# Bias products moved into the waits of the agents' chain, two more sets of products of ones, another order of loads, new sequences

## The chip, the core and the metric

The kernel runs on one NeuronCore of a Trainium2 chip. The metric is the device time of one execution in microseconds, and lower is better. TensorE (PE) multiplies matrices, with a separate instruction to load the weights (PEld). VectorE (DVE), ScalarE (ACT) and GpSimd (POOL) work on vectors. SyncE (SP) issues every load and store to one DMA queue. Each engine runs its own list of instructions in order. The engines wait for one another, and for loads, by semaphores.

## What is computed

The reference takes x (32 sequences of 100 tokens with 256 features), a context (32 x 361 x 256) and two masks. It runs six layers, each added to its input and followed by a layer norm:

```
x = LN(x + agent_attention(x))           # "agents": a softmax over features, one over tokens, all 32 sequences
x = LN(x + cross_attention(x, ctx))      # "first", masks added as logarithms
x = LN(x + top_half_attention(x))        # "pick": gates, the 50 best tokens, 16 heads
x = LN(x + banded_attention(x))          # "local": 16 heads, biases a_bq, a_bk, a_bv, a_bo
x = LN(x + cross_attention(x, ctx))      # "second": biases c_bq, c_bk, c_bv, c_bo
x = LN(x + int8_projection(quant(x)))    # "quant"
```

Everything is in float32 but the last product. Because biases meet only weights, some products depend on constants alone and are computed once at the start:

- for the second cross attention, `wqk` = c_qT · c_kT and `wvo` = c_vT · c_o (the combined weights), and `wqbk`, `bqbk`, `bqk` from c_bk and c_bq (the first bias products);
- `bo1` = a_bv · a_o + a_bo (the second bias product) and `bvo` = c_bv · c_o + c_bo (the third).

## The kernel before

The 32 sequences are 16 pairs. Four streams, A to D, each take one pair per turn, in four turns. A stream has its own tiles in SBUF and two of the eight PSUM banks. Within a turn it goes through the stages mix, first, pick, local, second and quant. Each engine has one generator per stream (`tensor_turns`, `vector_turns`, `scalar_turns`, `gpsimd_turns`, `sync_turns`). A string in `ORDER` (from line 1410), one per engine, says whose step comes next. Each letter advances that stream's generator to its next `yield`. So the order of work on every engine is written out by hand or by a planner, and an engine that meets a wait in its list holds back everything behind it.

Ahead of the turns stands the agent attention of all sequences: `tensor_agents`, `vector_agents`, `scalar_agents`. It is one serial chain. Tokens arrive in eight slots of four sequences (`ld_x`). For each slot TensorE transposes the tokens (line 362, semaphores x0 to x15), VectorE multiplies them with w (line 878, ag0 to ag7), and TensorE adds the weighed tokens of the slot before (`weighed`, line 331). From the sums y comes a row (yr1), its columns (line 337, yT1), the key product with w_k0 (line 375), a softmax over features (kmax, kexp, krec, kn), its transposes (line 380, arT), a product with w_v0 (z), the logits over tokens (line 394, log), their exponentials (lexp) and transposes (col), weighed tokens again (u), columns (yT2), and the product with w_v0T (line 411, vec). VectorE scales this to `agent_v`, semaphore v (line 922).

Where TensorE would wait in this chain, `idle(n)` (line 343) lets it compute n products of ones that nobody reads. Each is 256 columns wide and is recorded as two passes. They stand ahead of the tokens, three before kn, two before lexp, one before yr2, and one at the end.

The first turn of C and D opens with the constants' products in `tensor_turns` (C: first bias products, `wqk`; D: second and third, `wvo`). VectorE takes them out of PSUM (lines 978 to 991), with the semaphore "bias" of `s.tensor["start"]` and `s.vector["start"]`, for which ScalarE's q of the second cross attention and three steps of GpSimd wait as well. After that, four rows of `agent_v` are spread for each stream's pair (line 511), for which mix waits.

`sync_first` issues the loads in this order: w_q0, the tokens, w_k0, w_v0 and w_v0T (`ld_wk`), all other constants of the start (`ld_c`), x_k and x_o, masks of A and B, x of all streams, masks of C and D, contexts of A and B, the constants of the later stages (`ld_const`, 16 transfers), then after u the contexts of C and D, whose rooms held tokens, and after v the store of `agent_v`.

Of the kernel before, what the change touches and what calls it, by code (L numbers as in the profile page):

```python
# [15 lines left out]
P = 128  # L16
# [33 lines left out]
class Steps:  # L50
# [8 lines left out]
    def up(self, name):  # L59
# [46 lines left out]
AGENT_TENSOR = "zero w " + " ".join(f"x{n}" for n in range(16)) + " y yT1 key arT z log col u sum yT2 vec"  # L106
AGENT_SCALAR = " ".join(f"x{n}" for n in range(16)) + " toke kexp lexp"
AGENT_VECTOR = ("ones zero w " + " ".join(f"ag{n}" for n in range(8)) + " tokd yr1 yT1 kmax krec kn aT zT tokr tok lmax acol acol2 "
                "yr2 rsum yT2 v")
# [10 lines left out]
def program(nc, ins, out):  # L120
    ctx = ExitStack()
    with ctx:
# [117 lines left out]
        for s in streams[0:2]:  # L240
            s.tensor["start"] = Steps(s.tensor["start"].sem, "rows")

# [49 lines left out]
        ld_w0, ld_wk, ld_c, ld_first, ld_const = (sem(n) for n in ("ld_w0", "ld_wk", "ld_c", "ld_first", "ld_const"))  # L292
# [33 lines left out]
        def tensor_agents(e):  # L326
# [13 lines left out]
            def idle(n):  # L340

                for _ in range(n):
                    e.matmul(psum[0:S, 2, 0:D], ones[:, :], ones[:, 0:1].to_broadcast([P, D]), start=True, stop=True)

            e.wait_ge(*agent_dve("ones"))
            idle(1)
# [5 lines left out]
            idle(1)  # L352
# [16 lines left out]
            weighed(7, SLOTS - 1, token_w).then_inc(*agent_pe.up("y"))  # L369
            e.wait_ge(*agent_dve("yr1"))  # L370
# [6 lines left out]
            idle(3)  # L377
# [4 lines left out]
            e.wait_ge(*agent_dve("aT"))  # L382
            for h in range(NC):
# [5 lines left out]
            e.wait_ge(*agent_act("x15"))  # L389
# [7 lines left out]
            idle(2)  # L397
# [8 lines left out]
            idle(1)  # L406
# [6 lines left out]
            idle(1)  # L413

        def tensor_turns(e, s):
# [71 lines left out]
            for t in range(TURNS):  # L487
                if t == 0:

                    if s is SC_:  # L490
                        e.wait_ge(ld_c, LD_C)
                        spread(e, bk[0][:, 0:D], cols["c_bk"], W["c_qT"])
                        for c in range(NC):
                            e.matmul(bk[0][:, D:D + 1], cols["c_bk"][:, c:c + 1].to_broadcast([P, P]), cols["c_bq"][:, c:c + 1],
                                     start=c == 0, stop=c == NC - 1)
                        for h in range(NC):
                            last = columns(bk[0][:, D + 1 + h:D + 2 + h], W["c_kT"], h, lambda c: cols["c_bq"][:, c:c + 1])
# [202 lines left out]
        def scalar_turns(e, s):  # L700
# [16 lines left out]
            def cross(t, stage, bq):  # L717
# [3 lines left out]
                if t == 0 and bq is not None:  # L721
                    e.wait_ge(*SC_.vector["start"]("bias"))
# [136 lines left out]
        def vector_agents(e):  # L859
# [49 lines left out]
            e.tensor_tensor(tok[:, :], toke, tokr, ALU.mult).then_inc(*agent_dve.up("tok"))  # L909
            e.wait_ge(*agent_pe("log"))  # L910
# [3 lines left out]
            e.tensor_copy(acol.rearrange("p (i j) -> p i j", j=ROWS), batches(psum[0:S, 7, 0:P])).then_inc(*agent_dve.up("acol2"))  # L914
            e.wait_ge(*agent_pe("u"))
# [3 lines left out]
            batch_columns("yT2")  # L919
            e.wait_ge(*agent_pe("vec"))  # L920
# [3 lines left out]
        def vector_turns(e, s):  # L924
# [50 lines left out]
            for t in range(TURNS):  # L975
                if t == 0 and s is SC_:
                    e.wait_ge(*s.tensor["start"]("bias"))
                    e.tensor_scalar(wqbk[:, :], bk[0][:, 0:D], INV, None, ALU.mult)
                    e.tensor_scalar(bqbk[:, :], bk[0][:, D:D + 1], INV, None, ALU.mult)
                    e.tensor_scalar(bqk[:, :], bk[0][:, D + 1:D + 1 + NC], INV, None, ALU.mult).then_inc(  # L980
                        *s.vector["start"].up("bias"))
                elif t == 0 and s is SD:
                    e.wait_ge(ld_c, LD_C)
                    e.wait_ge(*s.tensor["start"]("bias"))
                    e.tensor_scalar(bq4[:, :], cols["a_bq"][:, :], HEAD_SCALE, None, ALU.mult)
                    e.tensor_copy(w8[:, :, :], w8_i)
                    e.tensor_tensor(bo1[:, :], bk[0][:, 0:D], rows["a_bo"], ALU.add)
                    e.tensor_tensor(bvo[:, :], bk[0][:, D:2 * D], rows["c_bo"], ALU.add).then_inc(*s.vector["start"].up("bias"))
# [205 lines left out]
        def gpsimd_turns(e, s):  # L1194
# [30 lines left out]
            for t in range(TURNS):  # L1225
# [17 lines left out]
                else:  # L1243
                    e.wait_ge(*SD.vector["start"]("bias"))
# [6 lines left out]
                if t == 0:  # L1251
                    e.wait_ge(ld_const, LD_CONST)
                    e.wait_ge(*SD.vector["start"]("bias"))
# [9 lines left out]
                if t == 0:  # L1263
                    e.wait_ge(*SC_.vector["start"]("bias"))
# [40 lines left out]
        def sync_first(e):  # L1305
# [16 lines left out]
            for n in COLVECS[1:]:  # L1322
# [15 lines left out]
            load_ctx(e, SB_, 0)  # L1338
            for n in ("f_q", "f_k", "f_v", "f_o", "a_q", "a_k", "a_v"):
# [7 lines left out]
            e.wait_ge(*agent_pe("u"))  # L1347
            for s in (SC_, SD):
                load_ctx(e, s, 0)
# [62 lines left out]
        "BACDABABCBCADADBCBAABDCAACABCDCBCBDADDACDDABABCAABBACADCBBACDABBCACDBDCBCABCDDADCBDAADACBDBDAACBACAC"  # L1412
        "DCBDBCABDDBCACBACBDCBABCCBCDADCDACDBABCADBCDABACADCBCADBCABDDABDCDADBADAAAADABCBBDBCBBABABCCDCDCCDCC"
        "BAABADDDADADBDBACCAABBABBCCDBDBCABACACACCDCCDAABDBBDCBABBADDDCDDACBCADBACDCDBDCBCABDDCACADBADCADBDBA"
        "BCDACCBADCACBBDBDCADBCDCABCABDADBCDBAACDABCADBDCABDCABCADCABBCBDDAACBADCADCAABCBAABABCDDCDBBBDBCBDAA"
        "DCCDCCBBCDACADDDAADDBAACACBAABBBBBBCDCDBACAACACCCCDCDBADBABDBACDDDDADCBBACACBDCCADBDCBDBACBDDCADCABD"
        "ACDBBCDADBCBAACACDBACBDBDCBACADCADBBCBADDBDCAADCABCABDDCBDAABCADBCADCDCBADBACCBACADBCABAAAADDBCBBDCD"
        "BBABBCACCDDCCDCABCBADADADDAADDCACABABBBBBBDCDCBACABACACDCCCCDAABDBABDDBCADDDDABBCACBCBDCABDCDBDACCBD"
        "DCAACBDADCADBDAABDACBCABDCCBCBDBADACDCBCDACBBADDBDACBCADACBBADCDABDABACCDCABCBDDBDCABCADCADCABDAAAAA"
        "BCDBCDBCBBBBACDCBDACDCCCDDDDDDBBCCDD"),  # L1420
    "DVE": (
        "BACBDCDCADABAABCBCCAADABDDACBABADCBCBDDCBCAACAAADADBABDACBABBBCBABCCBDCCCCDBDCDDADDDADAACBADABCBAABC"
        "DCBCBACBBDCADCCBABACDBCDCDBACDADBCAABDCABCBACDACABCDDBDBBDDDAAACDCAADABABBADBDBBCCACACBBCDCBDCDAABAD"
        "DCDCADABBCBDABDABACABCCDACABCCBABDCACDDABBACBABBDADBDCADDBCDACBCBDCCCDCBDCDDAADDDAADCBDABCBABCABACCD"
        "BDCBDCBADACBCADABDBACBDADCAABDCCBDABCBADACADBCCBDBBAADCACCDCDAABBADBDDBDBAABACCCBADBCBDCDCBADCAADCDA"
        "CDAABBBCDABBADACCBCDAACBCBCBDCDAAACDCADBBDAADBABDBDCCDCBBBACBDCDCCCBDCDDADDDCADBAADBCABACBACBACBDCBA"
        "BDCADBDCBACDABDABDDCACABDACCBDABBADADCACDBCCDBBBCACAADDCCAAABDBBDDAABDBBCCACBACBCDBCDADBAACDCDDACAAD"
        "CBBBDADABACDCBACBCCABCBABDCDACADCABDAADBDABBDBCDBCBBDABCCDCCDCCBDDCADDDADCAADBADABCBABCACBCDBADCBBCD"
        "DACBCADABDBCABDADCABACDCBADBACDDBCACBDBCDCBDDCAAACADAABDBADBCCABCBBABDCDCCDBDDDBCDCDCD"),
    "ACT": (  # L1430
        "ABBAABCDACCBABADBCABDCACCBDBACDDCDAADBADBCACBABADADBCCAABBACDDBBCCADCBACDABDDCABDAABDCACDCDBCBABBDAA"
        "CCCDBBDBCCACDAADCBBCBDDCADAABCCCABBADDAADBABDDABAAACDCBBACABBBCBACDCDDCBCADBCADABAADCDBDACADABBCABDB"
        "CDBBCCBBDCAACCADCACDACBDBDDCABCDBBDADABDBCCADCDABDDCBACDBCACDADBCABDDBACDACCABDBCDBBACDCDACABBDBDCDA"
        "CAACBBDBDDAACCABCABBDDADCACAACBAABABCADBBCBDCDBBAABDCCDADBBCCDACDCBDAADBDAACDACBAABCDABDBBCBBBACCDAC"
# [101 lines left out]
```

## Time and profile before

| what | value |
|---|---|
| runs | 853.36, 854.22, 847.25 us |
| median | 853.36 us |
| the profiled execution | 853.0 us |
| its span in the trace | 851.1 us |
| busy: PE, DVE, ACT, POOL | 92%, 77%, 57%, 42% of the span |
| mean granted clock of TensorE | 0.97 of full speed |
| chain that ended last | PE 64%, DVE 16%, POOL 8%, ACT 7% |
| DMA | 53.31 MB, mean 63 GB/s |

The profiled execution lies 0.4 us below the median. Its span leaves out 1.9 us around the recorded instructions. A busy share is an average over the whole run: the share of the first stretches differs from that of the rest, so it is read stretch by stretch. The granted clock is the share of TensorE's full clock (2.4 GHz) that it was given.

### The profile page before, as it was taken

To read this page: it belongs to the slowest core of one execution; us is meant where nothing else is said; L and a number is where in the kernel's file an instruction comes from. 1 tells how busy PE (TensorE), PEld (TensorE's weight loads), DVE (VectorE), ACT (ScalarE), POOL (GpSimd) and SP (SyncE) were. 2 spreads that over 40 slices of the span, in tenths; PEclk is the share of its full clock that TensorE was granted. 3 is DMA by queue.
4 is the path that set the end of the run, shared out by engine and by line. 5 is a ranking of instruction groups with operands and counts; after the bars stand their busy time and mean duration, and the time that the engine had idled before them with its cause. 6 is when DMAs were issued, how large, how long until landed. Compare 5 with 4: busy or idle time off the path is not lost.

```text
span 851.1 us, 20772 instructions
## 1 busy us (share of the span) xinstructions
PE 785.4 (92%) x8013; PEld 606.1 (71%) x8013; DVE 654.7 (77%) x1973; ACT 488.7 (57%) x1509; POOL 359.3 (42%) x604
## 2 busy tenths in 40 slices
PE   8989999998887999999989899999999899999992
PEld 4566787765766778766767688776777688777771
DVE  6163888787787698788778779789769879888676
ACT  3126445686556445577655554588655645587654
POOL 0088312306676523403775632402777633202465
PEclk7799999999999999999999999999999999999996
DMA  9893000001353000000236000001244200000001
GB/s 222 240 288 154 2 2 2 1 3 56 113 191 135 23 2 2 1 3 29 97 134 220 29 12 2 1 2 29 60 170 154 78 2 2 2 2 2 2 1 39
DMA packets 23074, 53.31 MB, mean 63 GB/s; under 512 B 3888, under 2 KB 9680, under 8 KB 22976
## 3 DMA queue, kind: packets, MB, share of 16 engines
q1 hardware_dynamic: 22976, 51.99, 19.1%
q8 instruction: 63, 1.03, 0.5%
q14 instruction: 35, 0.29, 0.1%
HBM read 48.67 MB, written 3.31 MB: 61 GB/s over the span
## 4 chain that ended last, share of the span: by engine, by line
PE 64%; DVE 16%; POOL 8%; ACT 7%; issue 3%; DMA 1%; SPq 0%; DVEq 0%; ACTq 0%; POOLq 0%
PE psum L429 11%; PE psum L434 11%; PE psum L473 8%; PE psum L630 5%; PE psum L652 5%; PE psum L459 4%; PE psum L643 4%; DVE bn L930 2%; ACT x L710 2%; POOL rstd L1199 2%; PE psum L466 2%; PE psum L565 2%; POOL xplus L1206 1%; PE psum L424 1%; PE psum L574 1%
## 5 line engine op out<-in xcount | busy, mean ns | idle before, releaser
L710 ACT ACTIVATE x<-res,ez,rstd 100x256 f32<-100x256 f32 x160 | 86.7, 593 | 65.4 <-POOL ez L1202 65.2
L473 PE MATMUL psum<-eT,ctx 128*128 128x100 f32 x768 | 95.2, 280 | 1.3 <-DVE eT L956 1.3
L473 PEld LDWEIGHTS psum<-eT,ctx 128*128 128x128 f32 x768 | 92.4, 197 | 2.5 <-DVE eT L956 1.7
L1197 POOL TENSOR_SCALAR ve<-mv 100x2 f32<-100x2 f32 x96 | 22.4, 233 | 163.2 <-DVE mv L933 159.1
L704 ACT ACTIVATE eT<-psum 100x400 f32<-100x400 f32 (+3 forms) x128 | 61.7, 495 | 43.7 <-PE psum L466 19.5
L459 PE MATMUL psum<-ctxT,qT 128*100 128x361 f32 x256 | 84.9, 474 | 1.5 <-ACT qT L704 1.1
L816 ACT ACTIVATE work<-psum,mx 100x100 f32<-100x100 f32 x256 | 67.5, 365 | 21.7 <-DVE mx L1112 21.5
L1185 POOL TENSOR_TENSOR kT<-cell,kT 100x722 f32<-100x722 f32 x12 | 20.7, 1722 | 131.5 <-ACT cell L684 131.5
L704 ACT ACTIVATE xT<-psum 128x400 f32<-128x400 f32 (+2 forms) x80 | 35.5, 445 | 69.0 <-PE psum L589 25.7
L1199 POOL TENSOR_TENSOR rstd<-ve,minus_half 100x2 f32<-100x2 f32 x96 | 70.1, 730 | 8.0
L930 DVE BATCH_NORM_STATS2 bn<-res 100x6 f32<-100x256 f32 x192 | 71.2, 412 | 0.0
L822 ACT ACTIVATE work<-psum,mx 100x100 f32<-100x100 f32 x256 | 67.9, 383 | 3.7 <-DVE mx L1115 3.6
L643 PE MATMUL psum<-ident,work 100*100 100x100 f32 x512 | 60.8, 255 | 3.1 <-ACT work L822 1.8
L459 PEld LDWEIGHTS psum<-ctxT,qT 128*100 128x100 f32 x256 | 41.3, 168 | 31.2 <-ACT qT L704 1.8
L1122 DVE RECIPROCAL xT<-psum 128x100 f32<-128x100 f32 x64 | 49.6, 776 | 14.6 <-PE psum L652 14.1
L1202 POOL TENSOR_SCALAR ez<-mv,rstd 100x1 f32<-100x1 f32 x192 | 52.9, 291 | 9.5
L643 PEld LDWEIGHTS psum<-ident,work 100*100 100x100 f32 x512 | 45.7, 128 | 14.6 <-issue 4.1
L466 PE MATMUL psum<-ident,work 100*128 100x100 f32 x192 | 29.0, 264 | 16.2 <-ACT work L741 15.8
L1112 DVE TENSOR_REDUCE mx<-psum 100x4 f32<-100x400 f32 x64 | 36.0, 568 | 9.3 <-PE psum L635 9.2
L1216 POOL COPY work<-rden 128x256 f32<-128x256 f32 x16 | 6.4, 398 | 84.2 <-DVE rden L1072 84.1
L1119 DVE COPY eT<-psum 100x400 f32<-100x400 f32 x64 | 35.8, 566 | 6.9 <-PE psum L643 6.4
L466 PEld LDWEIGHTS psum<-ident,work 100*128 100x128 f32 x192 | 20.8, 144 | 27.2 <-ACT work L741 23.9
(243 smaller groups left out, 2028.1 us busy)
## 6 DMA issues: line engine op xcount, KB each, us to landing
ctx<-in_ctx SPq DMA_DIRECT2D x16, 768.0 KB, 7.0
ctxT<-in_ctxT SPq DMA_DIRECT2D x16, 722.0 KB, 5.0
cell<-in_cell SPq DMA_DIRECT2D x12, 282.0 KB
seq<-in_seq SPq DMA_DIRECT2D x12, 282.0 KB
x<-in_x SPq DMA_DIRECT2D x16, 200.0 KB
out<-vs SPq DMA_DIRECT2D x16, 200.0 KB
eT<-agent_rows SPq DMA_DIRECT2D x12, 200.0 KB
work<-in_x SPq DMA_DIRECT2D x4, 384.0 KB
```

What stands on the lines that cost most here:

```text
L429: last = e.matmul(dst, w[:, c, h * P:(h + 1) * P], n(c), start=c == 0, stop=c == NC - 1)
L434: last = e.matmul(dst, xT(c), w[:, c, :], start=c == 0, stop=c == NC - 1)
L459: last = e.matmul(bk[b][0:S, 0:S2], s.qT[:, c, b * S:(b + 1) * S], s.ctxT[:, b, c, :], start=c == 0, stop=c == NC - 1)
L466: last = e.transpose(bk[b][:, j * S:(j + 1) * S], s.p[:, b, j * P:(j + 1) * P], ident[0:S, 0:S])
L473: last = e.matmul(bk[b][:, c * S:(c + 1) * S], s.ctx[:, b, j, c * P:(c + 1) * P], s.pT[:, b, j, :], start=j == 0, stop=j == S2C - 1)
L643: last = e.transpose(bk[g][0:S, q * S:(q + 1) * S], s.e[:, 4 * g + q, :], ident[0:S, 0:S])
L704: return e.activation(dst, src, ACT.Copy, **kw)
L710: e.activation(dst[0:S, b, :], s.res[0:S, b, :], ACT.Identity, scale=s.rstd[:, b:b + 1], bias=s.shift[:, b:b + 1]).then_inc(*act.up(f"x{b}"))
L816: last = e.activation(s.e[:, h, :], bk[0][0:S, h % 4 * S:(h % 4 + 1) * S], ACT.Exp, bias=s.mx[0:S, h:h + 1])
L822: last = e.activation(s.e[:, h, :], bk[1][0:S, h % 4 * S:(h % 4 + 1) * S], ACT.Exp, bias=s.mx[0:S, h:h + 1])
L930: e.bn_stats(s.bn[:, b, :], s.res[0:S, b, :]).then_inc(*dve.up(f"bn{b}"))
L1199: e.tensor_tensor(s.rstd[:, :], s.vare[:, :], minus_half[0:S, 0:NB], ALU.pow).then_inc(*pool.up("rstd"))
```

## The change

- `bias_c`, the first bias products, moves from C's first step into the wait for kn, in PSUM bank 4. It replaces three products of ones. The wait for x15 moves ahead of it. VectorE takes the results out after `tok`, semaphore cb.
- The second bias product moves from D's first step into the wait for lexp (bank 2, replacing two products of ones, semaphore ab). The third moves into the wait for yr2 (bank 3, replacing one, semaphore vb). VectorE does the casts and additions that belong to them after acol2 and after yT2.
- C and D keep the combined weights and the rows. The waits for "bias" are replaced by waits for cb, ab and vb.
- Two products of ones are added in the first slot, between its transposes and those of the second, and one between y and yr1.
- The loads: c_bq, c_bk, c_qT and c_kT (`ld_cb`) come directly behind w_k0, then w_v0 and w_v0T (`ld_wv`), then the rest of `ld_c`. The contexts of C and D, with their wait for u, come ahead of the constants of the later stages.
- All five strings of `ORDER` are new. They have the same lengths. A stream's n-th step moves by at most 7 places on PE, 5 on DVE, 8 on ACT, 7 on POOL and 3 on SP. POOL's first 20 steps are the same.

```diff
-            def idle(n):
+            def idle(n, bank):
...
+            def bias_c():
+                spread(e, psum[:, 4, 0:D], cols["c_bk"], W["c_qT"])
+                for c in range(NC):
+                    e.matmul(psum[:, 4, D:D + 1], cols["c_bk"][:, c:c + 1].to_broadcast([P, P]), cols["c_bq"][:, c:c + 1],
+                             start=c == 0, stop=c == NC - 1)
+                for h in range(NC):
+                    for c in range(NC):
+                        last = e.matmul(psum[:, 4, D + 1 + h:D + 2 + h], W["c_kT"][:, c, h * P:(h + 1) * P],
+                                        cols["c_bq"][:, c:c + 1], start=c == 0, stop=c == NC - 1)
+                last.then_inc(*agent_pe.up("cb"))
...
-                if i:
+                if i == 0:
+                    idle(2, 2)
+                else:
                     e.wait_ge(*agent_dve(f"ag{i - 1}"))
                     weighed(7, i - 1, token_w)
             e.wait_ge(*agent_dve("ag7"))
             weighed(7, SLOTS - 1, token_w).then_inc(*agent_pe.up("y"))
+            idle(1, 2)
             e.wait_ge(*agent_dve("yr1"))
...
-            idle(3)
+            e.wait_ge(ld_cb, LD_CB)
+            e.wait_ge(*agent_act("x15"))
+            bias_c()
             e.wait_ge(*agent_dve("kn"))
...
             e.wait_ge(*agent_dve("aT"))
+            e.wait_ge(ld_wv, LD_WV)
...
-            idle(2)
+            e.wait_ge(ld_c, LD_C)
+            spread(e, psum[:, 2, 0:D], cols["a_bv"], W["a_o"]).then_inc(*agent_pe.up("ab"))
             e.wait_ge(*agent_act("lexp"))
...
-            idle(1)
+            spread(e, psum[:, 3, 0:D], cols["c_bv"], W["c_o"]).then_inc(*agent_pe.up("vb"))
             e.wait_ge(*agent_dve("yr2"))
...
+                    e.wait_ge(*agent_dve("v"))
                     if s is SC_:
-                        e.wait_ge(ld_c, LD_C)
-                        spread(e, bk[0][:, 0:D], cols["c_bk"], W["c_qT"])
...
-                        last.then_inc(*s.tensor["start"].up("bias"))
                         weights(W["c_qT"], W["c_kT"])
                     elif s is SD:
-                        e.wait_ge(ld_c, LD_C)
-                        e.wait_ge(*agent_dve("v"))
-                        spread(e, bk[0][:, 0:D], cols["a_bv"], W["a_o"])
-                        spread(e, bk[0][:, D:2 * D], cols["c_bv"], W["c_o"]).then_inc(*s.tensor["start"].up("bias"))
                         weights(W["c_vT"], W["c_o"])
-                    if s in (SC_, SD):
-                        e.wait_ge(*s.vector["start"]("bias"))
-                    e.wait_ge(*agent_dve("v"))
...
-            for n in ("w_k0", "w_v0", "w_v0T"):
-                weight(n, ld_wk)
-            for n in ("a_o", "c_qT", "c_o", "c_kT", "c_vT"):
+            weight("w_k0", ld_wk)
+            for n in ("c_bq", "c_bk"):
+                e.dma_start(cols[n][:, :], ins[n]).then_inc(ld_cb, 16)
+            for n in ("c_qT", "c_kT"):
+                weight(n, ld_cb)
+            for n in ("w_v0", "w_v0T"):
+                weight(n, ld_wv)
+            for n in ("a_o", "c_o", "c_vT"):
                 weight(n, ld_c)
...
+            e.wait_ge(*agent_pe("u"))
+            for s in (SC_, SD):
+                load_ctx(e, s, 0)
             for n in ("f_q", "f_k", "f_v", "f_o", "a_q", "a_k", "a_v"):
                 weight(n, ld_const)
...
-            e.wait_ge(*agent_pe("u"))
-            for s in (SC_, SD):
-                load_ctx(e, s, 0)
...
-        "BACDABABCBCADADBCBAABDCAACABCDCBCBDADDACDDABABCAABBACADCBBACDABBCACDBDCBCABCDDADCBDAADACBDBDAACBACAC"
+        "BACDABBABCCDADABCADCABAACACBBCBDBDCADDACDDABABCAABCABADCBBACABBDCACDBDCABCBDDCACDBDAADACBDBADABCACAD"
...
```

## Rows read from the trace of the kernel before

**Rows 1.** The page, busy time of one engine over the span.
```profile
PE 785.4 (92%) x8013; PEld 606.1 (71%) x8013; DVE 654.7 (77%) x1973; ACT 488.7 (57%) x1509; POOL 359.3 (42%) x604
```

**Rows 2.** Busy time by stretch: us, each engine's busy time, granted clock, DMA.
```profile
4.27:7.69 3.42, 2.17 (x12) 1.28 (x11) 0.80 (x4) 0.00 (x0) 0.00 (x0) 1.00 1.05 248
7.69:11.10 3.41, 1.98 (x23) 1.17 (x22) 2.65 (x17) 1.80 (x4) 0.00 (x0) 1.00 1.06 234
11.10:28.17 17.07, 16.51 (x106) 8.99 (x106) 9.38 (x50) 6.17 (x13) 0.00 (x0) 0.50 0.99 253
28.17:31.58 3.41, 3.10 (x7) 1.53 (x8) 0.75 (x3) 0.56 (x2) 0.00 (x0) 0.50 0.61 203
45.45:57.27 11.82, 11.82 (x58) 8.92 (x58) 7.67 (x24) 2.07 (x4) 8.85 (x12) 1.00 0.94 297
57.27:72.62 15.35, 11.84 (x60) 8.30 (x60) 8.76 (x25) 9.07 (x24) 14.57 (x17) 1.00 0.82 295
72.62:93.00 20.38, 20.38 (x137) 17.08 (x138) 10.62 (x41) 10.70 (x34) 11.93 (x13) 1.00 0.09 30
93.00:837.13 744.13, 698.57 (x7375) 546.83 (x7373) 601.70 (x1763) 451.96 (x1418) 315.68 (x545) 0.99 0.13 45
```

**Rows 3.** Chain of waits, agents' chain: start us, us, what was waited for.
```profile
25.10 1.87 PE psum L331 x16
...
27.47 0.70 PE psum L337 x2
...
28.48 1.92 PE psum L375 x4
30.39 2.09 PE psum L343 x6
...
37.45 1.04 PE psum L343 x4
...
43.85 1.05 PE psum L411 x4
```

**Rows 4.** Timeline of the token slots: start us, us, instructions, idle time before them.
```profile
9.24 0.91 PE L362 MATMUL psum<-ident,work 100*128 100x100 f32 x8 [1.09 <-DMA work<-in_x]
...
21.50 0.08 DVE L878 DVE_READ_ACCUMULATOR x<-ctxT,vs 100x1 f32 x1
```

**Rows 5.** Chain of waits, first steps of C and D.
```profile
47.43 1.06 PE psum L323 x4
48.49 0.34 PE psum L494 x4
48.83 2.73 PE psum L429 x16
...
52.59 1.92 PE psum L323 x8
54.51 1.73 PE psum L429 x8
```

**Rows 6.** Timeline around the start of the streams, four instructions.
```profile
44.94 0.47 DVE L922 TENSOR_SCALAR agent_v<-psum,vs 32x256 f32<-32x256 f32 x1 [1.14 <-PE psum L411]
...
54.73 1.08 ACT L710 ACTIVATE x<-res,ez,rstd 100x256 f32<-100x256 f32 x2
...
63.93 2.60 PE L459 MATMUL psum<-ctxT,qT 128*100 128x361 f32 x8
...
71.52 0.54 DVE L943 CUSTOM_DVE_ANT_0 work<-psum,kT 100x361 f32<-100x361 f32 x1 [0.16 <-POOL kT L1185]
```

**Rows 7.** Timeline of SyncE's issues: the load of c_kT, B's context.
```profile
14.74 2.90 SPq L1307 DMA_DIRECT2D xplus<-in_c_kT  x1
...
38.00 0.49 SPq L1302 DMA_DIRECT2D ctx<-in_ctx  x1
```

**Rows 8.** The same two issues in the DMA view: KB, us to landing.
```profile
xplus<-in_c_kT SPq DMA_DIRECT2D x1, 256.0 KB, 9.4
...
ctx<-in_ctx SPq DMA_DIRECT2D x1, 768.0 KB, 20.0
```

More of the change, by code:

```diff
@@ L103 @@
 }
-AGENT_TENSOR = "zero w " + " ".join(f"x{n}" for n in range(16)) + " y yT1 key arT z log col u sum yT2 vec"
+AGENT_TENSOR = "zero w " + " ".join(f"x{n}" for n in range(16)) + " y yT1 key cb arT z log ab col u sum vb yT2 vec"
 AGENT_SCALAR = " ".join(f"x{n}" for n in range(16)) + " toke kexp lexp"
-AGENT_VECTOR = ("ones zero w " + " ".join(f"ag{n}" for n in range(8)) + " tokd yr1 yT1 kmax krec kn aT zT tokr tok lmax acol acol2 "
-                "yr2 rsum yT2 v")
+AGENT_VECTOR = ("ones zero w " + " ".join(f"ag{n}" for n in range(8)) + " tokd yr1 yT1 kmax krec kn aT zT tokr tok cb lmax acol acol2 "
+                "ab yr2 rsum yT2 vb v")
 def take(order, programs):
@@ L241, in program @@
             s.tensor["start"] = Steps(s.tensor["start"].sem, "rows")
+        for s in streams[2:4]:
+            s.tensor["start"] = Steps(s.tensor["start"].sem, "weights rows")
+            s.vector["start"] = Steps(s.vector["start"].sem, "weights")
         def job_before(s, t):
@@ L290, in program @@
         psum = ctx.enter_context(nc.psum_tensor("psum", [P, 8, 512], F32))
-        ld_w0, ld_wk, ld_c, ld_first, ld_const = (sem(n) for n in ("ld_w0", "ld_wk", "ld_c", "ld_first", "ld_const"))
+        ld_w0, ld_wk, ld_wv, ld_cb, ld_c, ld_first, ld_const = (
+            sem(n) for n in ("ld_w0", "ld_wk", "ld_wv", "ld_cb", "ld_c", "ld_first", "ld_const"))
         ld_x = [sem(f"ld_x{k}") for k in range(SLOTS)]
@@ L338, in columns_of_rows @@
                 return last
-            def idle(n):
+            def idle(n, bank):
                 for _ in range(n):
-                    e.matmul(psum[0:S, 2, 0:D], ones[:, :], ones[:, 0:1].to_broadcast([P, D]), start=True, stop=True)
+                    e.matmul(psum[0:S, bank, 0:D], ones[:, :], ones[:, 0:1].to_broadcast([P, D]), start=True, stop=True)
+            def bias_c():
[8 more added lines that the diff above has]
+                last.then_inc(*agent_pe.up("cb"))
             e.wait_ge(*agent_dve("ones"))
-            idle(1)
+            idle(1, 2)
             e.wait_ge(*agent_dve("zero"))
@@ L351, in tensor_agents @@
             last.then_inc(*agent_pe.up("zero"))
-            idle(1)
+            idle(1, 2)
             e.wait_ge(ld_w0, LD_W0)
@@ L369, in tensor_agents @@
             weighed(7, SLOTS - 1, token_w).then_inc(*agent_pe.up("y"))
+            idle(1, 2)
             e.wait_ge(*agent_dve("yr1"))
@@ L412, in tensor_agents @@
             last.then_inc(*agent_pe.up("vec"))
-            idle(1)
+            idle(1, 5)
         def tensor_turns(e, s):
@@ L721, in cross @@
                 if t == 0 and bq is not None:
-                    e.wait_ge(*SC_.vector["start"]("bias"))
+                    e.wait_ge(*agent_dve("cb"))
                 e.wait_ge(*pe("q", t))
@@ L914, in vector_agents @@
             e.tensor_copy(acol.rearrange("p (i j) -> p i j", j=ROWS), batches(psum[0:S, 7, 0:P])).then_inc(*agent_dve.up("acol2"))
+            e.wait_ge(ld_c, LD_C)
+            e.tensor_scalar(bq4[:, :], cols["a_bq"][:, :], HEAD_SCALE, None, ALU.mult)
+            e.tensor_copy(w8[:, :, :], w8_i)
+            e.wait_ge(*agent_pe("ab"))
+            e.tensor_tensor(bo1[:, :], psum[:, 2, 0:D], rows["a_bo"], ALU.add).then_inc(*agent_dve.up("ab"))
             e.wait_ge(*agent_pe("u"))
@@ L919, in vector_agents @@
             batch_columns("yT2")
+            e.wait_ge(*agent_pe("vb"))
+            e.tensor_tensor(bvo[:, :], psum[:, 3, 0:D], rows["c_bo"], ALU.add).then_inc(*agent_dve.up("vb"))
             e.wait_ge(*agent_pe("vec"))
@@ L975, in vector_turns @@
             for t in range(TURNS):
[L976 to L988, printed above, removed]
                 if t == 0 and s in (SC_, SD):
@@ L1243, in gpsimd_turns @@
                 else:
-                    e.wait_ge(*SD.vector["start"]("bias"))
+                    e.wait_ge(*agent_dve("vb"))
                 e.memset(s.v_pick[:, :, :, :], 0.0).then_inc(*s.gpsimd["pick"].up("zero"))
@@ L1252, in gpsimd_turns @@
                     e.wait_ge(ld_const, LD_CONST)
-                    e.wait_ge(*SD.vector["start"]("bias"))
+                    e.wait_ge(*agent_dve("ab"))
                 add_row(s.gpsimd["local"], s.scalar["pick"], t, bo1)
@@ L1263, in gpsimd_turns @@
                 if t == 0:
-                    e.wait_ge(*SC_.vector["start"]("bias"))
+                    e.wait_ge(*agent_dve("vb"))
                 add_row(s.gpsimd["second"], s.scalar["local"], t, bvo)
@@ L1321, in sync_first @@
                 e.dma_start(rows[n], ins[n].to_broadcast([P, D])).then_inc(ld_c, 16)
-            for n in COLVECS[1:]:
+            for n in ("a_bq", "a_bk", "a_bv", "c_bv"):
                 e.dma_start(cols[n][:, :], ins[n]).then_inc(ld_c, 16)
@@ new lines @@
+    "ACT": (
+        "ABABBACBCACDDACBABDACADCBADCBDCDBACADBBDACACDABDBACAABCABCBDABDCBACCBADCDABDADCBDBAADACCCDBCDABADBBA"
+        "CDCCBBBDCCCAADDABCCBCBDDAAABDCCCABBADDADABABDDAADAACBBCBCAABBBBACDCCDDCABCCBDADBAAADCDBDACADABCBADBB"
+        "DCBBBCCCDBAACDCACABCDCADBDDACBDCBADABCDDBBCADBCDADBDCADCCBACBDDADBACDBACBDAACCCDBDBBADCDACACBBDBDCDC"
+        "AABCADBDBDAACCABCBDABDACAADABCCAABBACABBDCBDCDBCBACADBDADBBCCDACDBCAADDABDACADCBAABCDABBDBCBBBACCDAC"
+        "CACCADBCCDADBDDCDBDCABADADBCABDBCDACDBCDBCABDCACDABDACBDDBCDCACABADBCBDACBDADCACBBBDDCDAAACCBDBDBADA"
+        "ACCBBCADBDADCACAABCBABADAACDBBCBCDBAABBCDCDACDBBDCACCADBAADABDACDCDAAABCBDDBCBBBABBCDCACCDACACDDCACB"
+        "BDDCABDCBDDBAADACDBBDCACBDDCBACCDBACDABDACBDADBAADCBCCDDBCBBACDACADCBBDDBCDAACACBBDBDADAACCCBBDDBDCA"
+        "CACAADBDAAABADCBCBBAACBCBCBDCDACDBDCBDADDDCCBDDCDBCD"),
```

61 lines of the change are left out of this document (25 added, 36 removed).

## The prediction

> **What bounds the kernel now.** I read the page first. TensorE is busy 785.4 of 851.1 us, 92% of the span [rows 1], so an edit counts if it takes work off TensorE or closes one of its 65.7 us of gaps. Then I asked for busy time by stretch, because the change touches the first 60 us and only reorders the rest. Three kinds of stretch stand there [rows 2]. Up to 45.45 us TensorE serves one serial chain of small steps (the agents' chain). From 11.10 to 31.58 the granted clock is 0.50, that is 1.2 GHz instead of 2.4, although TensorE is busy 16.51 of 17.07 us in the longest part of it. From 45.45 to 57.27 it is busy without a gap, from 57.27 to 72.62 it idles 15.35 - 11.84 = 3.51 us while GpSimd is busy 14.57 of 15.35, and from 72.62 to 93.00 it has no gap at all. After that it idles 744.13 - 698.57 = 45.6 us in 744, 6%. Third, the chain of waits gives the serial steps one by one [rows 3, 5]; the timeline gives the one wait for tokens that the change fills [rows 4]; two rows of other engines say what the start-up of the four streams hangs on [rows 6]; and the loads say when weights and contexts are there [rows 7, 8].
>
> The sum is made against the profiled execution: 853.0 us, span 851.1. The median of the runs shown is 853.36, so 0.4 us comes on top. Those runs go from 847.25 to 854.22: 1% (8.5 us) is about what a measurement of this kernel can tell from no change.
>
> **The change, part by part.**
>
> 1. Two products of ones in the first wait for tokens. One such product takes 1.04 / 2 = 0.52 us at full clock (two of them, the group at 37.45) [rows 3]; two make 1.04 us, and the wait they fill is 1.09 us [rows 4]: nothing is pushed back. What they might buy is the clock. Before it fell at 11.10, TensorE was busy 1.98 of 3.41 us, nearly all of it transposes of tokens and one set of weighed sums; one stretch earlier, with the products for w in it, it was busy 2.17 and kept full clock [rows 2]. After the fall it stayed at half for 17.07 us at 97% busy. So being busy with this mixture (a slot's transposes, then a set of weighed sums, the last two sets 1.87 us together at half clock [rows 3]) does not bring the clock back, and I see no reason why the same mixture, which leaves the engine less busy at full clock, should hold it. Two products come once; the mixture goes on for seven more slots. I take 0 for this part. The bound on the other side is the whole clock, and is rival one.
>
> The Trainium skill, "TensorE: Matmul & The Clock Gate", "Why this matters for your kernels", advises leaving no long idle gaps between bursts of matmuls so that the clock stays up; by that rule the filled wait keeps it and the result is the time of rival one. The trace speaks against this rule as the whole cause: the clock fell with no gap above 1.09 us ahead of it, and stayed down at 97% busy. The same page, "Part 4: PE-mode transpose", says that a transpose does not count as busy for the clock in the way a matmul does; that fits the row, and by it the products would have to outweigh the transposes of every slot.
>
> 2. One product of ones between y and the first column transposes. At half clock it takes 1.04 us; y ends at 25.10 + 1.87 = 26.97 and the transposes start at 27.47 [rows 3], so it pushes them to 28.0, +0.53. It may also let the clock return sooner. Before, the clock came back at 31.58, after the key product (1.92 at half clock) and the products of ones that start at 30.39. If it returns with the added product, at about 28.2: transposes 28.0 to 28.6, then 0.31 for VectorE (27.47 + 0.70 to 28.48), then the key product at full clock, 1.05 as its twin at 43.85 [rows 3], ends at 29.98. If it returns at 31.58 as before, the key product ends at 28.0 + 0.70 + 0.33 + 1.92 = 30.95.
>
> 3. The first bias products (`bias_c`) replace three products of ones (2.09 us, 30.39 to 32.48 [rows 3]) in the wait for kn. Their price at full clock: 1.06 + 0.34 + (2.73 - 1.73) = 2.40 us; the 2.73 holds the small products and the combined weights together, and 1.73 is the same combined-weight group alone, at 54.51 [rows 5]. Early return: 29.98 + 2.40 = 32.38, no later than before (-0.1). Late return: 0.6 us of it at half clock, the end at 33.68, +1.2. VectorE's three scalings follow while TensorE does transposes and logits, ahead of a maximum that is needed only once the logits are done.
>
> 4. The second (`ab`) replaces two products of ones, 1.04 us, by one pair, 1.06: 0. It waits for the other constants, whose loads of before were done when TensorE used them at 47.43 without a gap. The third (`vb`) replaces one product by 1.06: +0.54 if what follows had been waiting on the product rather than on VectorE, 0 if not; I take +0.54 [rows 3, 5]. VectorE's casts and additions lie under the weighed sums for u and the transposes behind them.
>
> 5. New waits on loads. c_kT landed at 14.74 + 9.4 = 24.1 [rows 7, 8]; now a_o and c_o are behind it and two 1 KB columns ahead. Nothing asks for it before 29.98. w_v0 and w_v0T slip behind it and are asked for after 32. Nothing paid; a whole weight's delay would still be covered.
>
> So agent_v, ready at 44.94 + 0.47 = 45.4 before [rows 6], comes between -0.1 + 0.54 = +0.4 and +1.2 + 0.54 = +1.7 us later. I take +1.1, the middle, since no row says when the clock returns.
>
> 6. After agent_v. Streams C and D lose their bias products: 2.40 and 1.92 us, 4.32 in all [rows 5]. The fourth stream's rows end 7.5 us after agent_v, not 11.8. But the first stage needs x of A and B, and ScalarE delivers it at 54.73 + 1.08 = 55.81 [rows 6], 10.4 after agent_v, whatever TensorE does: at that point only 57.27 - 55.85 = 1.4 of the 4.3 us is gained. GpSimd, 95% busy from there to 72.62 [rows 2], sets the softmax of the other stream (VectorE waited for its mask sum at 71.52 [rows 6]). What TensorE does ahead then counts, because it is the bound from 72.62 to 93.00. Contexts of C and D now come before the constants, so their scores can be drawn into the gaps. Bounds: 0 (everything hangs on GpSimd) and 4.3; I take 2.9, the middle between 1.4 and 4.3, nearer the upper end because a stretch of 20 us without a gap follows. The contexts wait for u behind those of A and B, as before; what is queued behind that wait are constants that the second stage is the first to use. The store of agent_v is still last: nothing paid.
>
> 7. The new sequences move steps by at most 7 places on TensorE, 5 on VectorE, 8 on ScalarE. Worth 0 by itself; bounds by the idle time they can act on, a tenth of 45.6: 4.6 us either way, of which I let 3 into the forecast's own range.
>
> **Sum.** 853.0 + 1.1 - 2.9 = 851.2, and 851.6 with the 0.4. Its own range: from 853.4 + 0.4 - 4.3 - 3 = 846.5 to 853.4 + 1.7 - 0 + 3 = 858.1.
>
> **The rivals.**
>
> *The clock holds through the tokens.* Then y is bound by arrivals: VectorE ends its last slot at 21.6 [rows 4]; one set of weighed sums (half of 1.87, and half of that again at full clock) later it is 22.1, 4.9 us ahead of 26.97. The column transposes gain 0.3 and the key product 0.87; `vb` costs 0.54, and `bias_c` about 0.3 over the products it replaces (2.40 - 2.09). agent_v is 4.9 + 0.3 + 0.87 - 0.84 = 5.2 us earlier. Then a load binds: the context of B lands at 38.00 + 20.0 = 58.0 [rows 7, 8], and its scores, at 63.93 before [rows 6], can gain 5.9, no more; what is done meanwhile for C and D can still gain up to 5.2 + 4.3 = 9.5 by work. I take the middle, 7.7: 845.7. For: the products fall where TensorE had its last long gap before the fall, and 847.25 among the runs before shows that something worth 6 us can go the other way. Against: rows 2. Chance 0.2.
>
> *The bias products lengthen the chain and give nothing back.* Place: the wait for kn, with the clock still down. At half clock `bias_c` is 4.8 us, 2.7 above the 2.09 replaced; with 0.53 and 0.54, agent_v is 3.8 us late. If GpSimd then sets the pace and only 1.4 us comes back: 853.4 + 3.8 - 1.4 = 855.8. It decides once agent_v is later than 45.4 + 2.9. For: GpSimd at 95%; added work where TensorE is slowest. Against: dense products brought the clock back at 31.58. Chance 0.15.
>
> *The sequences decide.* Fitted to the new state, they close a tenth of the later gaps and all of the 4.3 shows: 853.4 + 1.1 - 4.3 - 4.6 = 845.6, chance 0.1. Ill fitted by the same tenth: 853.4 + 1.1 - 2.9 + 4.6 = 856.2, chance 0.05.
>
> The forecast keeps 0.5.
>
> **Numbers.** The range takes the forecast's case but for its ends, half of rival one and most of rival two: 845 to 857. Faster by over 1%, below 844.8: the lower half of rival one with good sequences, 0.08. Slower by over 1%, above 861.9, needs rival two and bad sequences: 0.04. Within 1%: 0.88.
>
> **What would show it.** Step 1: the granted clock between 11 and 27 us; above 0.6 there I am wrong on the cause. Step 2: the end of the half-clock stretch, 28.2 or 31.6, and the start of the key product. Step 3: the transposes of the normalised key start between 32.4 and 33.7. Step 6: agent_v between 45.8 and 47.1, the last of the four rows 7.5 us behind it, then a gap of about 2.9 us until x is there; idle time of TensorE between there and 93. Step 7: TensorE's idle time after 93, against 45.6. The prediction is wrong if agent_v moves by over 2 us either way, or if the later idle time changes by over 5.

## The result, and the profile after

The changed kernel took 855.96 us (median of 20 runs, 851.17 to 860.13), the kernel before 852.33 us (20 runs, 844.65 to 858.68). The ratio is 1.006, interval 1.0037 to 1.0082: 0.6% slower. A ratio leaves out the executions that took over 1.5% more than the fastest of their kernel; medians and means take in all. The forecast was 851.6 us, a little faster. The time lies inside the range and within the 1% that was called the likeliest; the sign is wrong.

The profiled execution took 855.3 us, span 853.5. The page first, the engines' busy time:

```profile
PE 784.3 (92%) x8007; PEld 608.6 (71%) x8007; DVE 656.0 (77%) x1973; ACT 489.4 (57%) x1509; POOL 358.1 (42%) x604
```

TensorE is busy 1.1 us less and idle 3.5 us more than in [rows 1]. The busy time by stretch, columns as in [rows 2]:

```profile
4.27:7.69 3.42, 3.42 (x14) 2.21 (x13) 0.39 (x1) 0.04 (x1) 0.00 (x0) 1.00 1.00 258
7.69:11.10 3.41, 3.15 (x32) 2.21 (x29) 3.38 (x20) 1.93 (x5) 0.00 (x0) 1.00 1.06 257
11.10:28.17 17.07, 14.21 (x131) 8.66 (x130) 10.26 (x53) 6.00 (x15) 0.00 (x0) 0.98 1.00 259
28.17:31.58 3.41, 3.00 (x66) 2.73 (x70) 1.21 (x7) 0.00 (x0) 0.00 (x0) 0.50 0.63 184
45.45:57.27 11.82, 9.75 (x41) 7.11 (x40) 9.12 (x29) 3.34 (x7) 9.68 (x13) 0.90 1.03 356
57.27:72.62 15.35, 12.80 (x59) 9.02 (x59) 6.35 (x16) 10.83 (x31) 14.73 (x16) 0.97 0.69 236
72.62:93.00 20.38, 20.38 (x152) 17.73 (x151) 12.99 (x52) 9.19 (x28) 10.12 (x16) 1.00 0.09 29
93.00:837.13 744.13, 697.87 (x7345) 546.20 (x7343) 596.98 (x1742) 450.39 (x1410) 311.58 (x534) 0.99 0.13 45
```

From 11.10 to 28.17 the clock is 0.98 where it was 0.50, and TensorE, faster, is now less busy (14.21 us instead of 16.51). Then it is at half from 28.17 on. Here is the chain of waits of the agents' chain (start us, us, what was waited for), to be read against [rows 3]:

```profile
21.27 0.62 PE psum L335 x8
21.89 0.61 PE psum L347 x2
22.50 0.39 PE psum L341 x2
...
24.25 1.06 PE psum L327 x4
25.31 0.34 PE psum L352 x4
25.64 0.89 PE psum L356 x8
...
28.99 5.52 PE psum L414 x128
34.51 1.06 PE psum L327 x4
```

y is ready at 21.9 and not at 27.0. The bias products cost 1.06 + 0.34 + 0.89 = 2.29 us (2.40 foreseen). The logits (L414) then take 5.52 us at half clock. In the kernel before this row stood:

```profile
34.51 2.93 PE psum L394 x128
```

Two rows of the timeline give the end of the chain and the first product of the pick stage, the first work that needs the late constants:

```profile
42.33 0.47 DVE L940 TENSOR_SCALAR agent_v<-psum,vs 32x256 f32<-32x256 f32 x1 [0.81 <-PE psum L432]
...
87.19 0.42 DVE L1025 SCALAR_TENSOR_TENSOR work<-x,f_wg_r 100x256 f32<-100x256 f32 x1
```

The second of them in the kernel before:

```profile
90.33 0.43 DVE L1020 SCALAR_TENSOR_TENSOR work<-x,f_wg_r 100x256 f32<-100x256 f32 x1 [0.78 <-ACT x L710]
```

agent_v is there at 42.8 us, 2.6 earlier than in [rows 6]; the pick product starts 3.1 us earlier. So between these two profiles the start won 3 us, and the end is 2.4 us later by the two spans: 5.5 us are lost after 87 us. The idle time of TensorE after 93 us is nearly the same in the two profiles (46.3 and 45.6 us of a fixed stretch), so that count, which I had named as the sign to look at, does not show the loss: work that is late simply falls out of the stretch at its end. The timeline of SyncE's issues does show something, around 262 us:

```profile
260.04 0.35 SPq L1305 DMA_DIRECT2D ctxT<-in_ctxT  x1
260.44 0.43 SPq L1307 DMA_DIRECT2D ctx<-in_ctx  x1
260.91 0.36 SPq L1295 DMA_DIRECT2D eT<-agent_rows  x1
261.31 0.41 SPq L1305 DMA_DIRECT2D ctxT<-in_ctxT  x1
261.76 0.55 SPq L1307 DMA_DIRECT2D ctx<-in_ctx  x1
262.35 0.45 SPq L1295 DMA_DIRECT2D eT<-agent_rows  x1
262.91 0.31 SPq L1292 DMA_DIRECT2D x<-in_x  x1
```

The contexts of D and C (1.5 MB each) go out back to back, and C's x directly behind them. The kernel before, same view:

```profile
246.44 0.33 SPq L1300 DMA_DIRECT2D ctxT<-in_ctxT  x1
246.81 0.43 SPq L1302 DMA_DIRECT2D ctx<-in_ctx  x1
...
264.60 0.28 SPq L1287 DMA_DIRECT2D x<-in_x  x1
264.93 0.35 SPq L1300 DMA_DIRECT2D ctxT<-in_ctxT  x1
```

There C's context left at 246.44, and x led D's context. In the changed kernel SyncE stood still meanwhile. Its own waits from 215 to 285 us have this row, the wait of a context's load for D's second attention, over at 260 us:

```profile
SPq L1305 <- PE psum L494: 10.9, 1, 10.9
```

The chain of waits of the changed kernel goes on from there:

```profile
262.77 0.14 DVE work L1164
262.91 10.95 DMA x<-in_x
...
273.88 0.88 DVE res L1010 x2
```

x lands 10.95 us after its issue, and VectorE's mix waits for it. The same pattern stands at 434 us with B's context ahead of A's. In the view of waits from 100 to 837 us the kernel before has no wait for x at all; the changed one has this row:

```profile
DVE res L1010 <- DMA x<-in_x: 2.6, 2, 1.8
```

VectorE idles only 2.6 us for it, in two places, because it has other streams' steps to do first. The stream itself starts its turn late; what that costs in the end the row does not say, the experiments do.

### The profile page after: what moved, and what is told of

It reads as the page before. It is cut to its first block, busy times and chain, and to the rows that moved or that the text cites. A ratio compares the mean times of both kernels' runs of the same rounds, so it can differ in the third digit from the quotient of the medians.

```text
span 853.5 us, 20757 instructions
## 1 busy us (share of the span) xinstructions
PE 784.3 (92%) x8007; PEld 608.6 (71%) x8007; DVE 656.0 (77%) x1973; ACT 489.4 (57%) x1509; POOL 358.1 (42%) x604
## 4 chain that ended last, share of the span: by engine, by line
PE 65%; DVE 15%; POOL 6%; ACT 6%; DMA 4%; issue 2%; SPq 1%; DVEq 0%; ACTq 0%; POOLq 0%
PE psum L450 13%; PE psum L455 11%; PE psum L494 7%; PE psum L637 5%; PE psum L659 5%; PE psum L480 5%; PE psum L650 4%; DMA x<-in_x 2%; ACT x L717 2%; DVE bn L948 2%; POOL rstd L1204 2%; PE psum L572 2%; PE psum L581 2%; PE psum L445 2%; PE psum L555 2%
## 5 line engine op out<-in xcount | busy, mean ns | idle before, releaser
L1204 POOL TENSOR_TENSOR rstd<-ve,minus_half 100x2 f32<-100x2 f32 x96 | 71.9, 749 | 8.0
L659 PE MATMUL psum<-eT,v 100*32 100x100 f32 x1024 | 35.2, 254 | 5.0 <-DVE eT L1124 4.9
```

What stands on the lines that cost most here:

```text
L659: last = e.matmul(bk[bank][32 * r:32 * r + 32, 0:S], sums[:, j, :] if bank else s.v[0:S, b, c * HQ + h, :], s.eT[0:S, h * S:(h + 1) * S], ...
L1204: e.tensor_tensor(s.rstd[:, :], s.vare[:, :], minus_half[0:S, 0:NB], ALU.pow).then_inc(*pool.up("rstd"))
```

## The experiments

Each kernel was measured beside the kernel before on one chip, in five series. The series differ: the mean of the kernel before was 854.0, 849.6, 850.2, 850.2 and 851.0 us. So ratios are compared across series, times only within one.

**All old strings, and all new ones alone.** The first kernel is the changed one with the strings of `ORDER` of before, the second the kernel before with the new strings (a scheme of the edit, the strings left out):

```
 ORDER = {
-    # five strings of the kernel it starts from
+    # five strings of the other kernel
```

> The changed kernel with the five strings of ORDER of before; all else as changed. Theory one (the new sequences cost more, after the start, than the start gains): the start keeps its 3 us at 93 us and most of it reaches the end, 848 to 851, 1 to 4 us faster than before, and TensorE's idle time after 93 us stays near 45 us. Theory two (the loss comes from the moved products and loads, or from falls of the clock that any order has): 854 to 857, as the changed kernel.

Measured: 850.03 us against 852.96, ratio 0.9975 (0.9939 to 1.0012).

> The kernel before with the five new strings of ORDER and nothing else. Theory one: slower than before by 4 to 7 us (856 to 859), the loss coming after 93 us. Theory two: 851 to 854, within 1 us of before.

Measured: 860.41 us, ratio 1.0102 (1.0063 to 1.0141); by the means of all runs it is 859.86 - 853.96 = 5.9 us, 0.7%. The sequences cost; without them the changed kernel can't be told from the kernel before. Theory two falls.

**The products of ones.** Taken out of the changed kernel, and put alone into the kernel before:

```diff
-                if i == 0:
-                    idle(2, 2)
-                else:
+                if i:
...
             weighed(7, SLOTS - 1, token_w).then_inc(*agent_pe.up("y"))
-            idle(1, 2)
```

> The changed kernel without the two products of ones in the first slot and without the one behind y. If these products hold the clock through the tokens, it is at half again from 11 us, agent_v comes 3 us later or more (46 us instead of 42.8) and the time is 2 to 4 us above the changed kernel's, 858 to 860. If the clock held by chance, or the start is covered by GpSimd and loads, the time is that of the changed kernel within 1 us.

Measured: 858.20 us, ratio 1.0064 (1.003 to 1.0097). In its profile agent_v came at 49.3 us, and the clock from 11.10 to 28.17 was 0.67:

```profile
11.10:28.17 17.07, 14.69 (x110) 7.26 (x108) 9.35 (x52) 5.84 (x13) 0.00 (x0) 0.67 1.03 249
```

> The kernel before with only these three products of ones added (two in the first slot, one behind y). If they hold the clock: half clock gone between 11 and 28 us, agent_v some 5 us earlier (40.4 us), bounded by B's context at 58 us; time 2 to 5 us below before, 847 to 850. If they hold nothing: within 1 us of before.

Measured: 848.87 us, ratio 0.9985 (0.9954 to 1.0017). In its profile agent_v came at 40.3 us, with the clock at 1.00. The same kernel was run again later:

> The kernel before with the three products of ones alone, once more, beside the next two on one chip. If they are worth what they seemed: 3 to 5 us below before in the mean, and mean granted clock higher by 0.006 or more. If that was the chip's drift: within 1 us.

Measured: 848.67 against 849.68 us, ratio 1.0 (0.9964 to 1.0037), mean granted clock 0.9794 and 0.9793 for the kernel before. This time the profiled execution lost the clock in the same place. The first row is of the first series, the second of the later one, one and the same kernel:

```profile
11.10:28.17 17.07, 13.51 (x125) 7.31 (x125) 10.45 (x56) 6.03 (x15) 0.00 (x0) 1.00 0.96 242
```

```profile
11.10:28.17 17.07, 15.32 (x107) 7.57 (x105) 8.97 (x49) 5.74 (x13) 0.00 (x0) 0.65 1.00 251
```

So the products do not hold the clock for certain, nor does it always need them. Of the 16 profiles of kernels with them (one each, the changed kernel's among them), 12 had 0.98 or more in that stretch and four 0.80, 0.80, 0.65 and 0.60; of the four without, the kernel before had 0.50, the two named here 0.50 (all new strings) and 0.67 (no products), and a later one, with SyncE's new string alone, 1.00. That they help is likely; a gain in time is not shown.

That last profile says one thing more. SyncE's two strings differ only from their seventh step on, which comes after 230 us, so its start is that of the kernel before. It had agent_v at 40.4 us and the pick product at 86.60, against 45.4 and 90.33 in the kernel before, and 42.8 and 87.19 in the changed kernel. So the 3 us that the start seemed to win are less than what one and the same start differed by in two executions.

**Which turn's sequences.** New strings in about the first quarter of the steps, from there on, and in the second half (again a scheme):

```
-    k: new[k]
+    k: new[k][:c] + old[k][c:]      # e5, c near a quarter
+    k: old[k][:c] + new[k][c:]      # e6, c near a quarter; e7, near a half
```

> The changed kernel with the new sequences for the first quarter of each engine's steps and the sequences of before from there on. If the loss comes from the new order of the later turns (theory one, late): 848 to 851, as with all old sequences (850). If it comes from the new order of the first turn (theory one, early): 855 to 858, as the changed kernel.

Measured: 853.96 against 848.73 us, ratio 1.0042 (1.0008 to 1.0077).

> The changed kernel with the sequences of before for the first quarter of the steps and the new ones from there on. Late: 855 to 858. Early: 848 to 851. If both halves lose alike, this and the kernel that is new in the first quarter both lie near 853.

Measured: 854.72 us, ratio 1.0051 (1.0014 to 1.0087).

> As the last, with the new sequences only for the second half of the steps. Loss spread over all turns: about 852 to 853. Loss in the second quarter alone: 849 to 851. Loss in the second half: 855 to 857.

Measured: 855.63 us, ratio 1.0099 (1.0067 to 1.0131). All three are slower. The first two fit the case that both halves lose alike; but the last, with the fewest new steps, is slower than either, so the cuts do not locate the loss. Expanded into steps, SyncE's string has D's context ahead of C's only in the first of the three (x lands 10.54 us after its issue there), B's ahead of A's only in the second (9.21 us), and neither in the third, whose profile shows no such wait. So a loss of 1% also arises without either place. Much of it goes with the clock: the third ran at a mean of 0.9721, the kernel before at 0.9798, and among the runs of one kernel of this series the time changes by 0.66 us for each 0.001 of the mean clock. By that estimate 5.1 of its 6.5 us go with the clock. What lowered the clock there was not found; strings cut in two, which fit neither half's neighbours, may have done it.

**A product of ones behind z,** with all old strings:

```diff
             last.then_inc(*agent_pe.up("z"))
+            idle(1, 2)
```

> The changed kernel with all old sequences and one more product of ones behind z, where TensorE waits for the key weights and where the changed kernel's clock had fallen for 6.8 us (logits 5.5 us instead of 2.9). If that product keeps the clock: agent_v at about 40.5 us instead of 42.8, and 0 to 2 us off the 850 of the old sequences. If it does not, or if loads and GpSimd set the start: 850, or 0.5 above.

Measured: 851.97 us, ratio 1.0017 (0.9986 to 1.0048). The chain of waits of this kernel:

```profile
32.61 0.49 PE psum L347 x2
33.10 2.86 PE psum L415 x128
```

The logits are at full clock again, 2.86 instead of 5.52 us. But the clock had fallen among the tokens in this execution, so agent_v came at 44.3 us, no earlier. All profiles together bear the reading out. With the moved bias products and nothing behind z the logits took 4.3 to 5.5 us in eleven of twelve profiles and 2.9 in one (new strings in the second half). Without the moved bias products they took 2.9 in all six. With the product behind z, here and in a kernel further down, 2.9 in both.

**SyncE's string alone.**

```diff
     "SP": (
-        "ABCDAAABBDCCADBDCBCDBAABAACCDDCBDBCDAABBCDCBACDDBACD"),
+        "ABCDAABCABACDBCDDBCDAABBCADACBCDDBCDABABCACBDDDCBACD"),
```

> The changed kernel with only SyncE's string of ORDER as before; the four engines keep the new sequences. Theory one (the new order of SyncE's loads costs: two contexts stand ahead of a stream's x at 263 us, and x lands 10.95 us after its issue): the loss of the sequences, 6 to 7 us, goes for the most part, time 849 to 852, level with all old sequences, and no load of x over 5 us stands in the chain. Theory two (the order on TensorE, VectorE and ScalarE costs): 855 to 857 as the changed kernel.

Measured: 851.61 against 849.73 us, ratio 1.0021 (0.9994 to 1.0048), and no wait for x in its profile.

> The kernel before with only SyncE's string new. Theory one: slower than before by 4 to 7 us, as with all five new strings. Theory two: within 1 us of before.

Measured: 853.39 us, ratio 1.0043 (1.0001 to 1.0084). Here too x is waited for at 260 us, 10.72 us after its issue. So SyncE's string looks like part of the cost from both sides; the kernels that decide it come last.

> The changed kernel with SyncE's old string and one more product of ones behind z. If SyncE's string is the cost and the start's clock is worth something: the fastest of all, 846 to 849, 3 to 5 us below before. If the engines' sequences cost too: 852 to 855.

Measured: 850.92 us, ratio 1.0038 (1.0008 to 1.0068). Not the fastest: a miss.

**The contexts of C and D behind the constants again,** all old strings:

```diff
-            e.wait_ge(*agent_pe("u"))
-            for s in (SC_, SD):
-                load_ctx(e, s, 0)
             for n in ("f_q", "f_k", "f_v", "f_o", "a_q", "a_k", "a_v"):
...
+            e.wait_ge(*agent_pe("u"))
+            for s in (SC_, SD):
+                load_ctx(e, s, 0)
             e.wait_ge(*agent_dve("v"))
```

> The changed kernel with all old sequences and, in the first loads, the contexts of C and D behind the constants again. If the earlier contexts matter for the start: 1 to 3 us slower than the same kernel with them ahead (850 to 852 there, so 852 to 854), TensorE's gaps between 57 and 93 us larger by that. If GpSimd sets the pace there: within 1 us.

Measured: 854.89 us, ratio 1.0061 (1.0021 to 1.01). Slower than the same kernel with the contexts ahead (0.9975 above, 1.0037 below) in a comparison across series; its interval overlaps with the second of them. The sign that was named is missing: TensorE's idle time from 57.27 to 93.00 us is 2.23 us here and 2.23 us in the profile of the same kernel with the contexts ahead. Harm by the later contexts is not shown.

**The products of ones with the contexts ahead, and all old strings once more.**

> The kernel before with the three products of ones and the contexts of C and D ahead of the constants; bias products and sequences as before. If the moved bias products eat the start's gain: as the kernel with the products of ones alone, 3 to 5 us below before. If the earlier contexts do harm (they compete with masks and x): at before's level or above.

Measured: 848.74 against 849.68 us, ratio 1.0012 (0.9969 to 1.0055).

> The changed kernel with all old sequences, beside the last two. If the moved bias products and loads add nothing (TensorE's freed 4.3 us go to GpSimd's and ScalarE's pace and to clock falls at 28 and 52 us): 1 to 3 us above the kernel with the products of ones alone. If they pay: 1 to 3 us below it.

Measured: 850.62 us, ratio 1.0037 (0.9998 to 1.0077). Neither the moved bias products nor the earlier contexts can be told from no change.

**The two places of SyncE's string,** with the changed kernel and the old SyncE string beside it:

```diff
-        "ABCDAAABBDCCADBDCBCDBAABAACCDDCBDBCDAABBCDCBACDDBACD"),
+        "ABCDAAABBCCDADBDCBCDAABBAACCDDCBDBCDAABBCDCBACDDBACD"),
```

> The changed kernel with its own new SyncE string but for two places: in turn one C's context and x come ahead of D's context, in turn two A's context and x ahead of B's context. Theory one (a context that was ready stands behind one that is not, both go out together, and x lands 9 to 11 us after its issue): 2 to 4 us below the changed kernel in the same call, and as fast as with SyncE's whole string as before. Theory two (other places, or the engines' strings): within 1 us of the changed kernel.

Measured: 852.12 against 850.46 us, ratio 1.0034 (1.0003 to 1.0065).

> The changed kernel itself, beside the two others, to read them against: 855 to 857, 0.6% above before.

Measured: 857.08 us, ratio 1.0087 (1.005 to 1.0124).

> The changed kernel with SyncE's whole string as before. Theory one: 3 to 4 us below the changed kernel. Theory two: within 1 us of it.

Measured: 851.35 us, ratio 1.0021 (0.999 to 1.0051). By the means of twelve runs each, the two places are worth 857.05 - 852.56 = 4.5 us (within 2.6), the whole string 857.05 - 851.82 = 5.2 us (within 2.4). Not all of this is the wait itself: the mean granted clock is 0.9735 for the changed kernel and 0.9764 with the two places mended, and by the slope within this series, 0.58 us for each 0.001, 1.7 of the 4.5 us go with the clock (an estimate). SyncE's timeline with the two places mended:

```profile
262.95 0.30 SPq L1292 DMA_DIRECT2D x<-in_x  x1
263.30 0.35 SPq L1305 DMA_DIRECT2D ctxT<-in_ctxT  x1
263.69 0.43 SPq L1307 DMA_DIRECT2D ctx<-in_ctx  x1
```

x leads D's context, and no wait for x is left in this profile. By its ratio this kernel is still 0.34% slower than the one before.

## Why the prediction was wrong

**Step 1, the clock among the tokens: wrong.** I gave the products of ones nothing, because the clock had stayed down at 97% busy with the same mixture. That says what brings the clock back, not what takes it away. In the profile after, the clock held through seven slots. Rival one described this start. But even this is not certain from one execution to the next, as the two profiles of one kernel show, and no gain in time is shown. The Trainium skill, "TensorE: Matmul & The Clock Gate", "Why this matters for your kernels", advises against long idle gaps between bursts of matmuls. It hardly speaks to this case: the wait that was filled is 1.09 us [rows 4], and in the four profiles with that wait unfilled the clock was 0.50, 0.50, 0.67 and 1.00 from 11.10 to 28.17 us. The same page, "Part 4: PE-mode transpose", says that a transpose does not count as busy for the clock in the way a matmul does. It does not decide alone either, since the same mixture ran at 1.00 too, once without the products of ones.

**Steps 2 and 3: right in price, wrong in what follows.** `bias_c` cost 2.29 us. Nothing in the forecast said that it takes the place of dense products and is followed by small ones (z and the transposes), behind which the clock fell for the logits: 5.52 us against 2.93 before, 2.6 us, and slower than at full clock in eleven of the twelve profiles with the moved products and nothing behind z. One product of ones behind z gave 2.86. The foreseen sign, a late return of the clock after the tokens, did not arise.

**Steps 4 and 5: right.** `ab` and `vb` took 1.06 us each, and no wait for a weight stands in the chain.

**Step 6: too high.** agent_v was 2.6 us earlier and not 1.1 later, and the pick product 3.1 us earlier. Beyond agent_v the start thus kept 3.1 - 2.6 = 0.5 us of the 4.3, not 2.9. The gap foreseen ahead of the transposes of A and B is there, 1.07 us and not 2.9, and ScalarE's x sets its end:

```profile
51.15 2.08 ACT L717 ACTIVATE x<-res,ez,rstd 100x256 f32<-100x256 f32 x4 [15.93 <-POOL ez L1207]
...
51.81 1.87 PE L445 MATMUL psum<-ident,x 100*128 100x100 f32 x8 [1.07 <-ACT x L717]
```

The last of x comes 10.4 us behind agent_v, as in the trace before. The chain then shows where the rest went, in the sixteen products with the weights x_k. First the changed kernel, then the kernel before:

```profile
54.36 4.63 PE psum L450 x16
```

```profile
59.19 2.96 PE psum L429 x16
```

They start 4.8 us earlier, of which 2.2 is beyond agent_v, and end 3.2 earlier. In the changed kernel the clock is at half meanwhile, from about 55 to 58.3 us; in the kernel before it was at 1.00 during these products. The forecast gave this gap no price on the clock, and it was 1.7 us. It is no accident of one profile: from 45.45 to 72.62 us the mean clock is below 1.00 (0.87 or 0.94) in 18 of the 20 profiles, in all but the kernel before and the one with SyncE's new string alone.

Nor did the kernels with the old strings show a gain at the end that could be told from noise, where the forecast had 1.8 us for the start (1.1 later, 2.9 back). The profile of before had caught an execution with a low clock: 0.970 for the whole run, against 0.9735 to 0.9798 in the means of the later series. Part of the loss I read there was not there in most runs.

**Step 7, the sequences: the step that failed.** "Worth 0 by itself; bounds by the idle time they can act on": I looked at how far steps moved on the engines, and at SyncE's string not at all, though it moves loads of 1.5 MB. It is worth some 5 us of the 857 by the last series (5.2, within 2.4), most of it in two places (4.5, within 2.6). "Ill fitted by the same tenth", given 0.05 and 856.2 us, is what happened, but not by way of the engines' idle time: that the number is so near 855.96 is luck, and so is the hit of the range. How SyncE's order makes it: a step that must wait for a later event stands ahead of one that could go. D's context waits for D's second attention; C's stands behind it, though it had left at 246.4 us in the kernel before, some 14 us sooner; both leave from 260 us on, and x (200 KB) is issued while 3 MB are under way. The order could be read from the diff, by giving each letter its step: the new string has D's context, C's context, C's x where the old one has C's context, C's x, D's context (steps of other kinds between them left out).

**Open.** All new strings on the kernel before cost 1.02%, SyncE's alone 0.43%, with intervals that overlap; with SyncE's string as before, the engines' new strings on the changed kernel cost nothing that can be told (1.0021, twice; 1.0038 with the product behind z). Whether they cost on the old start is not settled. The profile with all new strings there had the pick product at 96.4 us, 6.1 later than in the kernel before and long before the two places, with a clock of 0.78 from 57.27 to 72.62; it is one profile. Nor is it known why new strings in the second half alone, with neither place in them, cost 1%, or what lowers the mean clock in the slower kernels.

## What to carry to other kernels

Read an order of DMA issues as an order of waits: a load that is ready must not stand behind one whose buffer comes free later, and the small load that the next turn needs goes out ahead of the large ones. When a table of orders changes, expand it into named steps and compare the queue that moves most bytes first. A serial start that ends sooner here met a wait for x, and behind it a clock at half; ask what stands behind a gain before counting it. And one profile of before does not say how the clock behaves in the median run.

## What the runs showed of the hardware

TensorE's granted clock differs between executions of one kernel. The same program had 1.00 and 0.65 of full speed from 11.10 to 28.17 us, and agent_v at 40.3 and 43.6 us. In the 20 runs of the changed kernel, time and mean granted clock go together (correlation -0.87; from 859.4 us at 0.968 to 851.7 at 0.977), so most of the scatter of 9 us between runs goes with the clock. And TensorE 97% busy at half clock, for 17 us of the kernel before, did not bring the clock back, while nearly the same work in the changed kernel, 83% busy, kept it at 0.98. A 200 KB load issued behind two contexts of 1.5 MB each landed after 10.95 us.
